# One row-maximum instruction instead of two per chunk, where the chunk's two PSUM banks are neighbours

## The reference, cut to what matters

```python
qkv = inputs @ W_qkv                                   # layernorm(x) goes in
score = jnp.einsum('bihd,bjhd->bijh', q, k) / D ** 0.5
mask = jnp.tril(jnp.ones((l, l)))[None, :, :, None]
masked_score = score * mask + 1e+30 * (mask - 1.0)
wmat = jax.nn.softmax(masked_score, axis=2)
out = jnp.einsum('bijh,bjhd->bihd', wmat, v).reshape(b, l, H * D)
x = x + out @ W_out
x = x + (h @ W.T + b + h @ lilora_weight.T)            # h = layernorm(x)
```

## Time and profile before

| | |
|---|---|
| median of 3 runs | 1908.71 us (1906.43 to 1910.15) |
| the profiled execution | 1910.15 us, its span 1908.1 us |
| PE busy | 1833.8 us, 96% |
| DVE busy | 1272.3 us, 67% (675.3 us of it are the 1200 reductions of L1017) |
| POOL busy | 972.8 us, 51% |
| ACT busy | 806.7 us, 42% |
| attention, about 317 to 1745 us | its stretch 300 to 1667 us: PE 1329.5 us, DVE 974.3 us, ACT 652.1 us, POOL 879.4 us busy |

### The profile page before, as it was taken

The page is one execution under the profiler, slowest core; times in us unless marked ns, Lnnn a source line. Parts: engine busy times, 40 slices in busy tenths (PEclk is TensorE's granted clock), DMA queues, the critical chain, the costliest instruction groups (busy, mean ns, idle before and its releaser), DMA issues. The chain is left out here.

```text
span 1908.1 us, 34290 instructions
## 1 busy us (share of the span) xinstructions
PE 1833.8 (96%) x13464; PEld 1128.0 (59%) x13464; DVE 1272.3 (67%) x2123; ACT 806.7 (42%) x982; POOL 972.8 (51%) x532
## 2 busy tenths in 40 slices
PE   7999998999999999999999999999999999998998
PEld 5877776555555555555555555555555555554897
DVE  5364652868676767676776767686777676747565
ACT  3222123454545454545454454545454545454221
POOL 1011000666675858575665666666758585746211
PEclk9999998999999999999999999999999999998999
DMA  5646445212121212222121312121212121023551
GB/s 204 223 179 232 164 157 210 68 35 78 41 73 46 72 46 68 62 58 67 46 74 51 80 45 79 40 74 46 67 46 73 46 68 51 24 73 102 177 192 56
DMA packets 150782, 171.33 MB, mean 90 GB/s; under 512 B 44618, under 2 KB 91744, under 8 KB 150624
## 3 DMA queue, kind: packets, MB, share of 16 engines
q1 hardware_dynamic: 150624, 169.15, 28.0%
HBM read 97.02 MB, written 71.57 MB: 88 GB/s over the span
## 5 line engine op out<-in xcount | busy, mean ns | idle before, releaser
L1017 DVE TENSOR_REDUCE f_part_max<-b_ring 128x1 f32<-128x512 f32 (+3 forms) x1200 | 675.3, 604 | 317.5 <-PE b_ring L850 213.5
L948 ACT ACTIVATE b_probs<-b_scores 128x1024 f32<-128x1024 f32 (+3 forms) x640 | 567.4, 898 | 615.5 <-PE b_scores L822 357.9
L1123 POOL TENSOR_TENSOR b_sum_pool<-b_sum_pool,b_probs 128x1024 f32<-128x1024 f32 x237 | 569.2, 2402 | 32.1 <-POOL b_sum_pool L1123 0.5
L1123 POOL TENSOR_TENSOR b_sum_pool<-b_probs 128x1024 f32<-128x1024 f32 x48 | 115.7, 2411 | 324.8 <-DVE g_sum_dve L1049 308.7
L822 PE MATMUL b_scores<-f_split 64*128 64x512 f32 (+2 forms) x1920 | 269.5, 383 | 9.1 <-ACT b_probs L948 7.3
L822 PE MATMUL b_scores<-b_split 64*128 64x512 f32 (+2 forms) x1920 | 268.0, 381 | 3.3 <-ACT b_probs L948 3.1
L886 PE MATMUL b_o_acc<-b_probs,f_v_in 128*64 128x512 f32 (+3 forms) x1280 | 270.5, 544 | 0.0
L886 PE MATMUL b_o_acc<-b_probs,b_v_in 128*64 128x512 f32 (+3 forms) x1280 | 269.0, 541 | 0.7 <-ACT b_probs L948 0.7
L1049 DVE TENSOR_TENSOR g_sum_dve<-g_sum_dve,b_probs 128x768 f32<-128x768 f32 (+3 forms) x243 | 229.5, 944 | 34.1 <-ACT b_probs L948 26.1
L822 PEld LDWEIGHTS b_scores<-b_split 64*128 64x128 f32 x1920 | 165.6, 185 | 51.0 <-issue 20.4
L822 PEld LDWEIGHTS b_scores<-f_split 64*128 64x128 f32 x1920 | 168.2, 187 | 46.0 <-issue 19.4
(11 more groups left out here) (135 smaller groups left out, 2288.5 us busy)
## 6 DMA issues: line engine op xcount, KB each, us to landing
f_raw<-k_t SPq DMA_DIRECT2D x32, 512.0 KB, 4.8
f_raw<-q_t SPq DMA_DIRECT2D x32, 512.0 KB, 5.6
g_recip<-r_t SPq DMA_DIRECT2D x128, 128.0 KB, 3.0
o_t<-g_o_norm SPq DMA_DIRECT2D x64, 256.0 KB, 2.0
q_t<-a_stage_a SPq DMA_DIRECT2D x32, 256.0 KB, 2.4
q_t<-a_stage_d SPq DMA_DIRECT2D x32, 256.0 KB, 2.0
k_t<-a_stage_a SPq DMA_DIRECT2D x32, 256.0 KB, 2.0
k_t<-a_stage_d SPq DMA_DIRECT2D x32, 256.0 KB, 2.0
```

Source lines behind the costliest of these rows:

```text
L948: nc.scalar.activation(probs[s % PR][:, :, off:], scores[s % 2][:, :, off:], ACT.Exp, scale=scale).then_inc(exp_done, 1)
L1017: nc.vector.tensor_reduce(part_max[:, h, ib, c:c + 1], rowwise[h][:, 0:width], AX.X, ALU.max).then_inc(chunk_reduced, 1)
L1123: nc.gpsimd.tensor_tensor(sum_pool[:], first, probs[s % PR][:], ALU.add).then_inc(pool_added, 1)
```

## The change

`reduce_chunk` gets the two bank numbers. Where the second follows the first, one `tensor_reduce` over [128, 2, width] writes two maxima per partition and counts `chunk_reduced` up by 2 at its end. Where they are (2,0), two instructions are issued as before.

```diff
-                def reduce_chunk(m, k, rowwise, turn):
+                def reduce_chunk(m, k, banks, turn):
                     ib, c = chunks[k]
                     width = min(TILE, (ib + 1) * P - c * TILE)
 
                     dve.wait_ge(chunk_made, m * CH + turn + 1)
+                    first, second = banks
+                    if second == first + 1:
+                        nc.vector.tensor_reduce(part_max[:, :, ib, c], ring[:, first:second + 1, 0:width], AX.X,
+                                                ALU.max).then_inc(chunk_reduced, 2)
+                        return
                     for h in range(2):
-                        nc.vector.tensor_reduce(part_max[:, h, ib, c:c + 1], rowwise[h][:, 0:width], AX.X,
+                        nc.vector.tensor_reduce(part_max[:, h, ib, c:c + 1], ring[:, banks[h], 0:width], AX.X,
                                                 ALU.max).then_inc(chunk_reduced, 1)
...
-                                reduce_chunk(n + 1, k, [ring[:, bank, :] for bank in ring_banks["chunk", k]],
-                                             turn_of[k])
+                                reduce_chunk(n + 1, k, ring_banks["chunk", k], turn_of[k])
```

## The result

| | median | runs |
|---|---|---|
| before | 1908.74 us | 1906.43 to 1910.15, 4 runs |
| changed | 1996.64 us | 1996.52 to 1997.55, 4 runs |

The ratio is 1.046, with a 95% interval of 1.0447 to 1.0473: 88 us slower. The profiled execution took 1997.55 us, its span is 1995.6 us.

What follows compares the result with a forecast made beforehand. PE sets the pace, held by the moment one bank comes free. Terms summed to 5.67 us per item, x 15 = 85.1 us on the profiled 1910.15 us: 1995.2, less 1.4 to the median, 1994 us; range 1965 to 2009 us.

Steps and rivals of the forecast that it cites:

- the term of the nine places: Nine merged 512-key chunks with one score unit before PE's next chunk: 0.526 us later each, 4.73 us per item.
- the late steps: Steps s8 to s10 and s20 to s22, where DVE is late: +0.38 and +0.19 us per item.
- the term of s30 and s32: Place 1 of steps s30 (256 keys) and s32 (384 keys): PE's next chunk +0.06 and +0.31 us later.
- Which place and which engine: PE waits for the first head's bank; merged, DVE releases it 1.216 us after the start instead of 0.69.
- if the distance from the end to PE's start stays: At the nine places, PE's matmul was assumed to keep starting 0.15 us after the releasing reduction's end: 0.526 us each.
- The chunks of place 2: Merged chunks followed by two value units: PE's loads 2.33 us apart, 1.91 needed, slack 0.42, nothing added.
- The stall is given back: Rival: PE stalls by 85 us, but existing waits vanish; if 25 us go, 1969 us; chance 0.10.
- Faster: Rival: DVE's chain sets the pace, so merging shortens the path: down to 1881 us, or 1905 us; chance 0.04.
- no difference: Rival: the 0.81 us is PE's own pace, the new end hides behind the score unit; 1909 us, chance 0.03.
- Costs more on the ring: Rival: the merged instruction takes 1.29 us like the pair; 15 us more, 2009 us; chance 0.03.
- The clock: Rival: TensorE's clock falls; a tenth of PE's time at half clock adds 133 us, 2127 us; chance 0.02.
- The rule that speaks for the change: Minimise the number of DVE operations: 405 fewer instructions should be a gain; the basis of the rival Faster.

Runs made afterwards that it cites:

- late_release: Kernel before with its two reductions, but at the 27 chunks with neighbouring banks the count rises by 2 at the second one's end: 1999.82 us.
- nine_only: Changed kernel with the merged instruction only at the nine named places of an item (135 instructions), pairs at the other 18 chunks: 1974.73 us.
- the two runs on the count: Changed kernel with merged reductions raising the count by 1: 1984.12 us; kernel before with each reduction raising it by 2: 1918.63 us.
- before_pool_later: Kernel before with one POOL multiplication per item (normalisation of the second query tile) moved from s22 to s25: 1896.61 us (ratio 0.9934).
- merged_counted_by_one: Changed kernel, but a merged reduction raises the count by 1 instead of 2, waits numbered anew: 1984.12 us (ratio 1.0396).
- merged_where_free: before_pool_later with merged reductions, counted by one, at the eight 512-key chunks with neighbouring banks that are followed by value units: 1895.85 us.

## Why the prediction was right

The median came out at 1996.6 us, 3 us over the forecast and inside the range. The mechanism is the one that was forecast. That the number came so close is partly luck: the term of the nine places was 11 us too low and that of the late steps 11 us too high, and these two errors cancelled; the term of s30 and s32 was 5 us too low.

- *Which place and which engine.* Right. The nine places were read off from one repeated distance, and all nine of them grew by the same amount. late_release shows the release as the cause by itself, nine_only that they carry most of the loss.
- *The term of the nine places* was 9 x 0.526 = 4.73 us per item and measured 5.44. The step that was short is "if the distance from the end to PE's start stays": it does stay, at 0.15, but the reduction starts 0.07 later (shown by the two runs on the count to come with the semaphore raised by 2) and takes 1.226 instead of 1.216. L447 in the earlier trace rows had the right length and could not show the start, since DVE never stood idle before it.
- *The terms of the late steps* were +0.38 for s8 to s10 and +0.19 for s20 to s22; measured +0.02 and -0.20. The arithmetic kept DVE's additions at their length beside POOL. But a delay of PE moves them against POOL's work, and at s20 the addition fell from 1.93 to 1.22 us. That the length at s20 comes from POOL is shown by before_pool_later. At s8 to s10 the same is only likely: the copy and the four additions there take 5.32 us of DVE's time instead of 5.59, but no run isolates it.
- *s30 p1 and s32 p1* were +0.06 and +0.31, measured +0.21 and +0.47. Both have the later start, and in both about 0.08 of the difference falls on the following distance: the next chunk's reduction starts 0.54 after its matmul instead of 0.46. That this is because PE had stood still before is an argument, not a test. It is seen in late_release and merged_counted_by_one too (0.54), so it does not come from the count.
- *The chunks of place 2* added nothing, as said. Their slack of 0.42 us was enough.
- *The rivals.* "The stall is given back": the wait for ACT stayed at 11.1 us, so not by ACT; what was given back lay in the late steps, whose distances came out 0.75 us per item under the sum; through POOL, as far as s20 is concerned. "Faster" and "no difference" fell at the nine places. "Costs more on the ring" held in a small way, mostly through the start; the length was 1.226, not 1.29. The clock stayed at 1.00.
- *The rule that speaks for the change* (the Trainium skill, "VectorE: DVE Perf Modes", section "Rules for kernel authors"), to minimise the number of DVE operations, gave no gain here even where it did no harm (merged_where_free).

In the profile after, the wait for the ring was forecast at roughly 100 us and is 100.8; DVE's busy time at 30 to 85 us less and is 34 less.

## What to carry to other kernels

Before two operations on a bottleneck's input buffers are merged, look at who waits for the first of them: a distance from one engine's end to another's start that repeats to the hundredth points to a release, as it did here, even if the wait list shows no hole there. Merge where nobody waits for the first part; elsewhere two instructions with two counts are a pipeline, and one is a barrier. And if an instruction both waits and raises a semaphore on the critical path, a step of 1 may be cheaper than a step of 2. Before a small delay is priced, look too at which operations of DVE and POOL it moves against each other.

## What the runs showed of the hardware that was not expected

- A DVE reduction that waits and raises its semaphore by 2 has its wait done by a separate instruction (405 of 405 and 600 of 600 cases) and starts 0.07 us later after the releasing matmul (0.61 against 0.54), in both directions of the test. It cost 12.5 us in the changed kernel and 10 us in the kernel before.
- A DVE addition with both inputs in SBUF took 1.93 us beside a POOL multiplication and 1.22 us alone. Moving one such multiplication by three steps made the kernel before 0.66% faster (ratio 0.9934), and that, not the merging, is the version here that beats both kernels.
